# Patch tokens, attention and a gated MLP in one program: an order of its own for the passage between the last patch step and the first attention groups, and VectorE for the cells' sum of the last step

## The reference

```
pe = conv(pixel_values, conv_w, stride 14)            # 9x9 cells per image, C = 256
red = mean over each 3x3 window of cells; win = its 9 cells
q = ln(red) @ la_wq;  k, v = ln(win) @ la_wkv          # 8 heads of 32
attn = softmax(q . k over the 9 cells);  agg = sum over the 9 cells of attn * v
local_out = red + agg @ la_proj_w;  patch_out = local_out @ mod_w
cls_out = class token, attending over the 9 windows
h = concat(patch_out, cls_out, txt)                    # 64 images x 87 tokens x 256
h = h + proj(attention(layernorm(h)))                  # 16 heads of 16, q and k normed and rotated
h = h + W_lin x + two of eight rank-4 adapters picked by a gate      # x = layernorm(h)
```

## Time and profile before

| | us |
|---|---|
| median of 3 runs | 750.31 (746.08 to 753.61) |
| the profiled execution | 748.84 |
| its span | 747.1 |
| PE busy / VectorE busy | 692.7 / 531.6 |

### The profile page before, as it was taken

How to read it: one execution, slowest core, us unless ns; L and a number is a source line. 1 busy time by engine, 2 the same in 40 slices (tenths; PEclk the granted TensorE clock), 3 DMA queues, 4 the chain that set the end, 5 groups by cost and what they waited for, 6 DMA issues and landing times.

```text
span 747.1 us, 23721 instructions
## 1 busy us (share of the span) xinstructions
PE 692.7 (93%) x9277; PEld 556.3 (74%) x9277; DVE 531.6 (71%) x1204; ACT 394.9 (53%) x969; POOL 422.0 (56%) x450
## 2 busy tenths in 40 slices
PE   5998998999976889999999999999999999999884
PEld 3987887888754667788788778778778787877652
DVE  2468687878883367787887877887878878866642
ACT  4553543535332256656666665656666565665431
POOL 3667572764657246567566575575575575663221
PEclk9999999999997699999999999999999999999976
DMA  8963562330110122223223223223222322122100
GB/s 220 235 155 114 148 199 47 81 69 28 38 42 16 31 70 69 64 71 74 78 72 75 83 70 77 80 68 78 78 72 71 83 74 73 41 58 56 37 19 27
DMA packets 69524, 58.69 MB, mean 79 GB/s; under 512 B 30607, under 2 KB 68646, under 8 KB 69286
## 3 DMA queue, kind: packets, MB, share of 16 engines
q1 hardware_dynamic: 69414, 57.18, 29.9%
HBM read 33.69 MB, written 11.40 MB: 60 GB/s over the span
## 4 chain that ended last, share of the span: by engine, by line
PE 73%; DVE 14%; issue 3%; ACT 3%; DMA 3%; SPq 2%; POOL 1%; POOLq 0%; DVEq 0%; ACTq 0%
PE p_a L1331 13%; PE p_c L1331 11%; PE p_s L1391 6%; PE p_o L1403 6%; PE p_conv L758 6%; PE p_kv L758 5%; PE p_c L1451 4%; PE p_s L1373 3%; PE p_n L1411 3%; PE p_mm L758 3%; PE p_a L1357 2%; PE p_s L1387 2%; PE p_c L1432 2%; DMA kr<-qkT 2%; DVE kv L656 2%
## 5 line engine op out<-in xcount | busy, mean ns | idle before, releaser
L1126 POOL TENSOR_TENSOR t<-t,ss_rs 116x512 f32<-116x512 f32 x48 | 50.9, 1060 | 126.4 <-ACT ss_rs L1173 125.2
L1266 DVE TENSOR_REDUCE mx<-p_s 87x16 bf16<-87x1392 f32 x64 | 101.6, 1587 | 24.6 <-PE p_s L1373 24.3
L1197 ACT ACTIVATE prT<-p_s 87x1392 f32<-87x1392 f32 x64 | 85.1, 1329 | 57.8 <-PE p_s L1391 56.3
L426 POOL TENSOR_TENSOR xs_lo<-xcols,xs_hi 120x585 fp32r<-120x585 f32 (+1 forms) x45 | 60.4, 1350 | 43.8 <-ACT xs_hi L483 43.8
L1120 POOL TENSOR_TENSOR t<-t 116x512 f32<-116x512 f32 x48 | 61.0, 1270 | 18.0 <-DVE t L1257 18.0
L1391 PE MATMUL p_s<-qr,kr 32*87 32x87 f32 x2048 | 67.9, 255 | 0.0
L1129 POOL TENSOR_TENSOR t<-t,tabs 116x512 f32<-116x512 f32 x48 | 62.9, 1310 | 3.8
L1391 PEld LDWEIGHTS p_s<-qr,kr 32*87 32x87 f32 x2048 | 59.5, 152 | 0.0
L1387 PE MATMUL p_s<-mxT,pick_row 32*87 32x87 bf16 x1024 | 55.4, 207 | 1.4 <-ACT mxT L1191 1.4
L1331 PE MATMUL p_c<-w_f,yT 128*116 128x296 f32 x184 | 56.0, 427 | 0.4 <-ACT yT L1216 0.4
L1403 PE MATMUL p_o<-prT,vp 87*32 87x87 f32 x2048 | 54.7, 246 | 0.0
(11 more groups left out here) (267 smaller groups left out, 1896.6 us busy)
## 6 DMA issues: line engine op xcount, KB each, us to landing
xcols<-in_x_cols SPq DMA_DIRECT2D x12, 822.7 KB, 8.0
h<-h_tokens SPq DMA_DIRECT2D x16, 348.0 KB
out<-out_sb SPq DMA_DIRECT2D x48, 116.0 KB
h_tokens<-in_txt SPq DMA_DIRECT2D x4, 1232.0 KB, 8.7
x<-in_txt_cols SPq DMA_DIRECT2D x32, 154.0 KB, 3.2
qr<-qkT SPq DMA_DIRECT2D x64, 58.0 KB, 2.2
kr<-qkT SPq DMA_DIRECT2D x64, 58.0 KB, 2.0
vp<-vt SPq DMA_DIRECT2D x32, 87.0 KB
```

The source lines that it names most:

```text
L426: nc.gpsimd.tensor_tensor(xs.lo[:, n % XS_SLOTS, :, 0:M].bitcast(F32R), raw, xs.hi[:, n % XS_SLOTS, :, 0:M], ALU.subtract).then_inc(S['xs_ ...
L1126: link(nc.gpsimd.tensor_tensor(t4, t4, ss_rs[:, b].unsqueeze(2).broadcast_to([TP, 2 * HEADS, HD]), ALU.mult))
L1197: nc.scalar.activation(prT[:, k % 2], p_s[0:SEQ, :, 0:QUADS * SEQ], ACT.Exp, scale=HD ** -0.5).then_inc(S['s_exp'], 1)
L1266: nc.vector.reduce_max(mx[:, k % 2, :, 0:QUADS], p_s[0:SEQ, :, 0:QUADS * SP].rearrange("p j (a k) -> p j a k", k=SP)[:, :, :, 0:SEQ], AX_X ...
```

## The change

The tables for steps and groups stay. Five new tables, one for each engine, give the steps w3, w4, g0 and g1 of the passage planned times of their own, and `play` uses them in place of the regular ones; all other steps keep theirs. Step 4 now sums its cells on VectorE as the others do. g0.xhi no longer waits for the last convolution (g0.rotate waits for the last `xs_lo` instead); g0.exp.0 and g0.hb.0 wait for w4's sum and not its transpose; `rstd_r` waits for `eps`, which may now come behind it; the clearing of two buffers on GpSimd become steps of their own (`strips`, `ones`). No operation is added or removed but for the sum and its 40 matmuls, which become two transposes.

```diff
+def passage(text):
+    return {(turn[0], int(turn[1:]), name, int(k)): int(time) for turn, name, k, time in (step.split('.') for step in text.split())}
-def play(windows, window_step, groups, group_step):
+def play(windows, window_step, groups, group_step, moved):
+    turns = {('w', s, name, k): WINDOW_PERIOD * s + time for s in range(STEPS) for name, k, time in windows}
+    turns.update({('g', g, name, k): GROUP_START + GROUP_PERIOD * g + time for g in range(GROUPS) for name, k, time in groups})
+    turns.update(moved)
...
-                if name == 'sum' and s < STEPS - 1:
+                if name == 'sum':
...
                 if name == 'aggT':
                     use('T', S['aggT_out'], s + 1)
-                    if s < STEPS - 1:
-                        pe_.wait_ge(S['agg'], s + 1)
-                        transpose(p_T, agg[0:M], M).then_inc(S['aggT'], 1)
-                    else:
-                        pe_.wait_ge(S['vw'], PIECES * (s + 1))
-                        for c in range(CC):
-                            part = slice(C + P * c, C + P * (c + 1))
-                            mm_ = mm(p_T[:, c, 0:M], [kv[0:M, ring(s, j), i, part] for j in range(PIECES) for i in range(LOAD_CELLS)]
-                                     + [bias_kv[0:1, part]], [ident[0:M, 0:M]] * CELLS + [consts.ones[0:1, 0:M]])
-                        mm_.then_inc(S['aggT'], 1)
+                    pe_.wait_ge(S['agg'], s + 1)
+                    transpose(p_T, agg[0:M], M).then_inc(S['aggT'], 1)
...
-                        pool.wait_ge(W['aggT'], STEPS)
+                        pool.wait_ge(W['agg'], STEPS)
...
-                    if g == 0:
-                        act.wait_ge(W['conv'], CONVS)
...
+                    if g < 2 and k == 0:
+                        act.wait_ge(S['eps_ok'], g + 1)
...
-                        act.wait_ge(W['aggT'], STEPS)
+                        act.wait_ge(W['agg'], STEPS)
...
+                        dve.wait_ge(W['xs_lo'], CONVS)
```

More of the change, by code:

```diff
@@ L223, in table @@
     return [(name, int(k), int(time)) for name, k, time in (step.split('.') for step in text.split())]
-def play(windows, window_step, groups, group_step):
[L228 to L231, removed]
+def passage(text):
[4 more added lines that the diff above has]
+    turns.update(moved)
+    for part, n, name, k in sorted(turns, key=lambda turn: turns[turn]):
+        (window_step if part == 'w' else group_step)(name, n, k)
 def take(engine, freed, banks, semaphore, n):
@@ new lines @@
+PASSAGE_DVE = passage("""w4.xlo.0.1692 w3.score.2.1727 w4.xlo.1.1731 w3.s_max.0.1731 w4.xlo.2.1739 g0.stats.0.1744 w3.att.0.1746
+                w4.xlo.3.1791 w3.sum.0.1807 w3.sum.1.1887 w4.xlo.4.1899 g0.stats.1.1906 w4.xlo.5.1908
+                g0.stats.2.1914 w3.lo.0.1917 w4.redb.0.1921 w4.red_var.0.1924 g1.stats.0.1927 w3.lo_var.0.1936
+                w3.patch.0.1962 w4.xlo.6.1979 g0.rotate.0.1985 g0.ss.0.1993 g0.eps.0.2006 w3.gv.0.2035
+                w4.xlo.7.2036 g1.stats.1.2048 w3.g_m.0.2050 w4.q.0.2056 w4.xlo.8.2059 w4.prod.0.2089
+                g0.rotate.1.2095 w4.q_kb.0.2109 w4.prod.1.2109 w4.score.0.2113 w4.score.1.2122 w4.prod.2.2123
+                g0.ss.1.2130 w4.score.2.2135 w4.s_max.0.2135 w3.g_att.0.2145 w4.att.0.2147 g0.rotate.2.2153
+                g1.stats.2.2182 g0.ss.2.2204 w3.gw.0.2225 w4.sum.0.2227 w4.sum.1.2233 g1.rotate.0.2243
+                w3.cls.0.2260 g0.max.0.2278 g1.eps.0.2289 w4.lo.0.2309 g1.ss.0.2325 g1.rotate.1.2329
+                w4.lo_var.0.2345 w4.patch.0.2367 g1.ss.1.2384 g0.max.1.2394 w4.gv.0.2430 w4.g_m.0.2449
+                w4.g_att.0.2458 g1.rotate.2.2459 g1.ss.2.2479 w4.gw.0.2535 g0.max.2.2545 g0.norm.0.2598
+                g0.norm.1.2609 g0.max.3.2621 w4.cls.0.2631 g0.h2.0.2666 g0.norm.2.2668 g1.max.0.2685
+                g1.max.1.2743 g0.stats_c.0.2776 g0.h2.1.2780 g0.norm.3.2781 g0.stats_c.1.2781 g1.max.2.2801
+                g0.h2.2.2830 g1.norm.0.2839 g0.stats_c.2.2875 g1.max.3.2905 g1.norm.1.2914 g1.norm.2.2954
+                g1.h2.0.2999 g0.logits.0.3015 g1.h2.1.3025 g0.rank.0.3054 g1.norm.3.3055 g0.weigh.0.3067
+                g1.stats_c.0.3076 g1.stats_c.1.3089 g0.out.0.3093 g0.out.1.3107 g0.out.2.3120 g1.h2.2.3141
+                g1.logits.0.3295 g1.rank.0.3484 g1.weigh.0.3510 g1.out.0.3574 g1.out.1.3577 g1.out.2.3596""")
@@ new lines @@
+PASSAGE_POOL = passage("""g0.xc.0.1427 w4.red.1.1622 w4.red.2.1665 w4.red.3.1689 w3.vw.0.1749 w3.vw.1.1767 w3.vw.2.1840 g0.xlo.0.1916
+                w4.red.4.1920 w4.red.5.1925 w4.red.6.1966 w4.red.7.1970 w4.red.8.1979 g0.strips.0.2007
+                g1.xc.0.2028 g0.add.0.2028 g0.scale.0.2035 g1.xlo.0.2043 g0.shift.0.2073 g0.add.1.2077
+                g0.scale.1.2080 g0.shift.1.2088 w4.vw.0.2107 w4.vw.1.2172 w4.vw.2.2182 g0.add.2.2184
+                g0.scale.2.2196 g0.shift.2.2210 g0.hb.0.2243 g1.add.0.2286 g0.ones.0.2306 g1.add.1.2426
+                g1.shift.0.2463 g1.scale.1.2497 g0.hb.1.2508 g1.shift.1.2524 g1.add.2.2537 g0.hb.2.2544
+                g1.scale.2.2585 g1.shift.2.2592 g1.hb.0.2722 g0.base.0.2952 g1.hb.1.2972 g0.above.0.3009
+                g1.hb.2.3035 g0.base.1.3100 g0.base.2.3118 g1.base.0.3281 g1.base.1.3287 g1.above.0.3288
+                g1.base.2.3407""")
@@ L935 @@
+PASSAGE_SP = passage("""w3.rows.0.1889 g0.place.0.2085 g0.place.1.2322 g0.values.0.2338 w4.rows.0.2352 g0.values.1.2415 g1.values.0.2431
+                g1.place.0.2651 w3.cls.0.2667 g1.values.1.2735 w4.cls.0.2741 g1.place.1.2752 g0.store.0.3030
+                g0.store.1.3419 g0.store.2.3427 g1.store.0.3487 g1.store.1.3527 g1.store.2.3591""")
 H_SLOTS = 4
@@ L1111, in step @@
                                           ).then_inc(S['x_ok'], 1)
-                    if g == 1:
-                        clear_strips()
+                if name == 'strips':
+                    clear_strips()
+                if name == 'ones':
+                    clear_values()
                 if name == 'xlo':
@@ L1120, in step @@
                     link(nc.gpsimd.tensor_tensor(t1[:, b], t1[:, b], t2[:, b], ALU.add))
-                    if g == 0 and k == 0:
-                        clear_values()
                 if name == 'scale':
@@ L1471, in _ @@
         def _(sp):
-            play(WINDOW_SP, windows[0](sp), GROUP_SP, groups[0](sp))
+            play(WINDOW_SP, windows[0](sp), GROUP_SP, groups[0](sp), PASSAGE_SP)
             for t in range(TILES):
@@ L1484, in _ @@
             link = counted(act, consts.S['act_1'])
-            play(WINDOW_ACT, windows[2](act, link), GROUP_ACT, groups[2](act, link))
+            play(WINDOW_ACT, windows[2](act, link), GROUP_ACT, groups[2](act, link), PASSAGE_ACT)
         @block.vector
@@ L1494, in _ @@
             freed = {}
-            play(WINDOW_PE, windows[4](pe, freed), GROUP_PE, groups[4](pe, freed))
+            play(WINDOW_PE, windows[4](pe, freed), GROUP_PE, groups[4](pe, freed), PASSAGE_PE)
 def arrays_of(inputs):
```

42 lines of the change are left out of this document (40 added, 2 removed).

## The result

| kernel | median, us | runs | ratio to before, 95% |
|---|---|---|---|
| before | 749.1 | 746.08 to 753.61 | 1 |
| after | 763.83 | 758.8 to 770.03 | 1.0199 [1.0138, 1.0259] |

The forecast was 734 us, faster; the kernel takes 2% longer, above the range. The profiled execution of after took 767.35 us with a span of 765.6, against the 748.84 and 747.1 of before: the traces differ by 18.5 us, the medians by 14.7, so some 4 us of what follows is one execution against another.

A forecast was written before the change was run, and what follows sets the result against it. PE bounds nearly everywhere except the passage from 201.1 to 281.2 us. Terms 202.1 + 8.5 + 21.3 + 9.8 + 1.4 + 18.5 + 2.4 + 1.5 put g2.qk.0 at 265.5, 15.7 us earlier: 734 us, range 723 to 746.

The forecast's parts named there:

- From g2.qk.0 on the same: Behind the passage: the 15.7 us gained at g2.qk.0 would stay unchanged to the end of the kernel.
- The step on SyncE: Passage DMA queue: g0.place.0 ahead of group 2's load of h makes VectorE wait 6 us, bounds 0 and 13.
- SyncE becomes the bound: Rival, 742 us, chance 0.14: slow value issues make g0.pv.1 wait 3 us; with 7 for the load, 8 us more.
- conv.8 ends at 202.1: Ahead of w4's last convolution: a later w4.xlo.1 delays its end by 1.0 us from 201.1, bounds 0 and 3.
- VectorE's leg, 21.3: From w4.xlo.7 at 210.6 to the end of w4's sum at 231.9: VectorE never waits, its operations take 21.3 us.
- contention: VectorE's two-operand operations stretched beside GpSimd in the passage: 1.5 us added, bounds 0 and 5.
- From w4.loT to g2.qk.0, 18.5: End of the passage on PE: 18.5 us, of which 0.9 idle, where before took 21.8 us busy.
- The clock: PE at half clock for at least 5 us behind six idle microseconds: +2.4 us, or +9 if it stays longer.
- The rival "half clock": Rival, 761 us, chance 0.05: spread waits keep PE at 1.2 GHz from g0.v.0 on; g2.qk.0 at 294, 12 us later.
- The sum, -9.3 + 0.4 on PE: w4's cell sum leaves PE, saving 9.3 us there, and two transposes add 0.4 us.
- 0.46 alone: First operation of w3.s_max on VectorE: said to take 2.89 us beside GpSimd and 0.46 without it.
- The signs of being wrong: g2.qk.0 beyond 275, PEclk 0.5 over 10 us, a PE wait over 4 us not loT's, changed period behind 281.

The follow-up runs named there:

- sum alone: The kernel before with only w4's cell sum moved to VectorE, all orders as before: 742.59 us, ratio 0.9857; second run 737.64 us, 0.9855.
- loads first: After with the six stores of g0 and g1 at old times, g0.place.0 and g1.values.0 behind the loads of groups 2 and 3: 745.93 us, 0.9925.
- front only: Stores back and the two loads ahead, and every passage step whose old time is 2700 or later at its old time on every engine: 737.81 us, 0.9836.
- end of group 1 back: Loads first, with g1's logits, rank, weigh, out, gate, twT, lora, above and base at their old times: 739.15 us, 0.9843.
- stores back: After with only the six stores of g0 and g1 at their old planned times on SyncE: 754.03 us, 1.0039.
- the sum on PE: Loads first, with w4's sum on PE again as 36 matmuls: 760.74 us, 1.0145.

## Why the prediction failed, step by step

- *"From g2.qk.0 on the same"*, and "I take the rest of the kernel as it was": **the step that failed.** I had followed SyncE's queue through the passage and not through the stores, which the same table moves too: they go out 57 and 118 us behind g2.qk.0. What I had put at nothing measured 20.9 us in the trace at g8. Of the 29.8 us between forecast and median the stores are 12 by the medians (9.4 behind g2.qk.0 by the traces), and the late end of group 1 that they wait for 6 more: 15 to 18.
- *The step on SyncE*: the mechanism (place.0 and values ahead of loads) was right and was worth 8.1 us. As a wait it was mis-sized in both directions: for group 2 I had 6 us and VectorE waited 1.74, being late itself (it came there at 246.9 and not at 235.8); for group 3, on which I put nothing, it waited 3.69, and PE 4.5 for vp and 2.9 in oN. The order of events was nearest to that of the rival "SyncE becomes the bound", which had g0.pv.1 wait 3 us for its values; here it was g0.pv.0.
- *"conv.8 ends at 202.1"*: at 205.8, 3.7 late. 2.2 of these were there before any changed step and are of this execution (the load of group 0 went out at 173.62 for 171.43; in later kernels with the same order up to there it is 170.1 to 171.7). The wait of w4.xT.3 was 1.66 us for my 1.0; and taking it away gained nothing.
- *"VectorE's leg, 21.3"*: w4.xlo.7 began at 214.87 and not at 210.6, and from there to the end of the sum at 240.0 it was 25.1. The list of operations was complete; all of the 3.8 us over it are operations that took longer than alone: two products 1.93 and 1.59 us for 0.94, the first two of the softmax 1.01 and 1.32 for 0.46 and 0.23, the sum 5.5 for 4.95. Of contention I had 1.5 with an upper bound of 5, so this term was 2.3 too low. The sum's reductions ran as alone (2.85 and 1.04), and the adds took 1.17 and 0.42. With the 3.7 us of conv.8 and 0.6 between, where the eps took 0.94 us for the 0.14 it takes elsewhere, this is the 8.1 us that the sum came late. The Trainium skill ("GPSIMD Engine Reference", Specifications) has GpSimd contend with VectorE's instructions that have two SBUF inputs. The trace agrees: the operations with two such inputs were held and the reductions were not (the eps, with one input, was held too). For the adds, held as long as L669 was, I had worked out 4.9 us; here it was 0.6, and the products of the same leg lost more.
- *"From w4.loT to g2.qk.0, 18.5"*: loT began at 249.87 for my 243.1 and g2.qk.0 at 279.73, 29.9 us behind it, with the waits for vp and oN in it. This is the largest miss inside the passage: 6.8 us late at loT, then 11.4 more, of which the terms for clock and contention cover 3.9, make the 14.2 us between 265.5 and 279.73. *The clock* had +2.4. It was at half from 227.7 to 248.2 us, behind waits of PE of 1.0 and 1.8 us, and again for some 7 us each from 258.4 on, in PE's wait for vp, and from 275.5 on, behind the one in oN; the mean from 240 to 281 was 0.75. The rival "half clock" had it so for its 761 us, though in one stretch and with g2.qk.0 at 294. That 761 lies near the measured 763.8 is chance: that rival had all of the loss inside the passage, where 1.5 us were gained.
- *The sum, -9.3 + 0.4 on PE*: right. The sum alone gave 10.7 us by the ratios and 8.8 in the trace at g8.
- *The rest of the gain*, the some 7 us that the order was to bring beside the sum: not there at the end, in no variant. With the loads first g2.qk.0 did come 11.8 us ahead of before, 3.5 more than with the sum alone, but at g8 only 1.8 were left.
- *"0.46 alone"* was a misreading of the earlier trace rows: at 226.59 GpSimd was at work as well, with a multiplication that began at 225.69 and took 1.26 us. L669 ended 0.10 us behind it. So what holds such an operation isn't that GpSimd works beside it, but how long GpSimd's own operation has still to go (last section).
- The chances: 0.05 for slower was far too low, since all the cases were about the passage and none about the steps behind it that the same tables move. The signs of being wrong were well chosen: g2.qk.0 came beyond 275, the half clock lasted over 10 us, PE waited over 4 us for something else than loT, and the period behind 281 us changed.

By the ratios, each step against the kernel that differs from it by that step: the sum -1.5%, the new order of the front -0.2% and of the tails +0.1%, both nothing within the intervals, the end of group 1 late +0.8%, places and values ahead of loads +1.1%, stores ahead of loads +1.6%. These kernels form one row from before to after, so that the steps must add up to 1.0199; what is shown is their size, each to some 0.5%. In the traces (one execution each, us; only at g8 have all done the same work):

| kernel | ratio | g2.qk.0 | g8.qk.0 | between |
|---|---|---|---|---|
| before | 1 | 281.21 | 451.33 | 170.1 |
| sum alone (second run) | 0.9855 | 272.94 | 442.58 | 169.6 |
| front only | 0.9836 | 271.11 | 442.09 | 171.0 |
| end of group 1 back | 0.9843 | 270.35 | 444.74 | 174.4 |
| loads first | 0.9925 | 269.42 | 449.56 | 180.1 |
| stores back | 1.0039 | 276.53 | 458.21 | 181.7 |
| after | 1.0199 | 279.73 | 470.76 | 191.0 |

## What to carry to other kernels

When an order is written by hand, list for each in-order queue, to its very end, every step that waits, and what stands behind it: above all a store ahead of a load on one DMA queue. A load that is due late in the program is lost to a store that looks harmless by its own time. And price an order by the one chain that leaves the passage last (here, as the rows suggest, att, vw, sum, tail), not by the idle time of the busiest engine: here idle time was filled without that chain moving, and nothing was gained.

## What was not expected of the hardware

- From its issue to the first instruction that reads it, the 348 KB load of `h` took 7.4 us (336.81 to 344.19) to 10.5 us (262.97 to 273.49) with VectorE standing; the longer one had six issues of vp ahead of it. From group 5 on, before gives such a load a lead of 9.4 to 10.5 us. An estimate from these numbers is a slack of 0 to 3 us: hardly any delay of its issue is hidden.
- Half clock came with short waits too. In after PE was busy 6.3 and 6.5 us in the slices 220:230 and 230:240, no wait over 2 us, and the granted clock fell from 0.88 to 0.50. With the sum on PE it was 0.50 from 240 to 250 us though PE was busy for all of the 10 us. The same was there in before: 0.50 from 237.7 to 255.1 us, PE busy 16.3 of 17.4, so that its 9.3 us of matmuls for the sum were at half speed.
- VectorE's held operations end a fixed time behind an operation of GpSimd. GpSimd in after, beside the two slow products shown above:

```profile
216.45 1.69 POOL L1183 TENSOR_TENSOR xT_lo<-x,xT_hi 128x696 fp32r<-128x696 f32 x1
218.11 2.01 POOL L1194 TENSOR_TENSOR t<-t,tabs 116x512 f32<-116x512 f32 x1
220.31 1.40 POOL L1187 TENSOR_TENSOR t<-t 116x512 f32<-116x512 f32 x1 [0.19 <-DVE t L1323]
```

  The first of these ends at 218.14 and the product at 218.96, the third at 221.71 and the product at 222.52: both some 0.82 us behind, nearly the 0.94 of a product alone. The second, begun while the first product was still to be done, took 2.01 us for its usual 1.27. So each stood for the other. It is no chance of these two. In the whole traces of before and after, 131 of VectorE's operations on two tensors in SBUF took over 0.08 us more than the shortest of their form. In each a TENSOR_TENSOR of GpSimd ended, and the operation ended a time behind it that is the same for its form: 0.81 to 0.82 us for the products, 0.27 to 0.28 for the adds of 256 columns, 0.08 to 0.09 for the softmax's of 72. A memset of GpSimd held nothing: in before a product at 215.20 took 0.95 us beside one that ran from 214.32 to 216.76.
- SyncE's six issues of values in after span 6.00 us, of which 1.7 are a wait: g1.values.0 waits for the transfers of g0.values.0 (its buffer's semaphore), and the load of group 3 stood behind that wait too. The issues themselves are 1.62 us for two and 2.63 for four. Directly behind a load of `h` the same four took 7.11 us in before, and 6.91 in the kernel with the loads first.
